# State-space layer: the softplus sum with an adding DMA, scans in place over four PSUM banks, and each read-out one unit later

## What is computed

```python
def _mamba(x, W_in, conv_w, conv_b, W_xproj, W_dt, b_dt, A_log, D_param, W_out):
    xp, z = jnp.split(x @ W_in.T, 2, axis=-1)           # 2 x 384 channels
    xc = silu(causal_conv4(xp) + conv_b)
    dt, Bt, Ct = jnp.split(xc @ W_xproj.T, [12, 28], axis=-1)
    dt = softplus(dt @ W_dt.T + b_dt)
    A = -jnp.exp(A_log)                                 # 384 x 16 states
    def step(h, inp):
        dt_t, B_t, C_t, x_t = inp
        h = jnp.exp(dt_t[..., None] * A) * h + (dt_t * x_t)[..., None] * B_t[:, None, :]
        return (h, jnp.einsum('bdn,bn->bd', h, C_t))
    _, ys = jax.lax.scan(step, h0, inputs)              # over the 128 tokens
    return ((ys + xc * D_param) * silu(z)) @ W_out.T
h = h + 0.5 * (_mamba(x) + _mamba(x[:, ::-1])[:, ::-1]) # x = layernorm(h)
```

## Time and profile before

| | us |
|---|---|
| median of 3 runs | 4825.98 (4822.94 to 4830.41) |
| profiled execution, its own time | 4824.94 |
| span of its trace | 4823.1 |
| PE busy | 4354.2 (90%) |
| DVE busy | 3395.9 (70%) |
| POOL busy | 3184.9 (66%) |
| ACT busy | 2378.0 (49%) |
| granted TensorE clock, mean | 0.959 of full |

### The profile page before, as it was taken

How to read it: one execution, slowest core, us unless ns; L and a number is a source line. 1 busy time by engine, 2 the same in 40 slices (tenths; PEclk the granted TensorE clock), 3 DMA queues, 4 the chain that set the end, 5 groups by cost and what they waited for, 6 DMA issues and landing times. The chain is left out here.

```text
span 4823.1 us, 62759 instructions
## 1 busy us (share of the span) xinstructions
PE 4354.2 (90%) x17088; PEld 2262.3 (47%) x17088; DVE 3395.9 (70%) x5016; ACT 2378.0 (49%) x4078; POOL 3184.9 (66%) x1637
## 2 busy tenths in 40 slices
PE   7999986996999999999999999999999975999994
PEld 4666644663334343343434334343433333666673
DVE  5677763111899999999999999999999985111114
ACT  3555542122665665656666565666656534122221
POOL 3222212441998999999999999999999951444441
PEclk9999997997999999999999999999999987999997
DMA  1000012342232233333223233222323221333456
GB/s 34 20 23 20 16 61 64 110 131 77 84 110 99 98 109 103 102 100 105 99 102 109 100 106 100 105 98 102 109 100 105 97 80 35 106 116 116 124 168 217
DMA packets 262442, 453.11 MB, mean 94 GB/s; under 512 B 38892, under 2 KB 175932, under 8 KB 262300
## 3 DMA queue, kind: packets, MB, share of 16 engines
q1 hardware_dynamic: 235776, 403.02, 25.3%
q0 software_dynamic: 23424, 48.00, 3.2%
q10 hardware_dynamic: 3100, 0.64, 0.1%
HBM read 409.75 MB, written 41.81 MB: 94 GB/s over the span
## 5 line engine op out<-in xcount | busy, mean ns | idle before, releaser
L1765 POOL TENSOR_TENSOR m_xh<-m_u,m_Bb 128x1536 f32<-128x1536 f32 x512 | 1753.0, 3457 | 223.4 <-DVE m_u L1639 223.0
L1694 PE MATMUL bank<-m_xh,ident 128*128 128x512 f32 x3072 | 1443.5, 605 | 26.3 <-POOL m_xh L1754 26.3
L1721 ACT ACTIVATE bank<-m_dt,m_Ac 128x508 f32<-128x508 f32 x1536 | 1019.2, 683 | 416.5 <-DVE bank L1736 281.1
L1736 DVE TENSOR_TENSOR_SCAN bank<-bank,m_xh 128x512 f32<-128x512 f32 x864 | 1060.1, 1227 | 36.3 <-ACT bank L1721 7.8
L1694 PEld LDWEIGHTS bank<-m_xh,ident 128*128 128x128 f32 x3072 | 568.5, 192 | 807.9 <-issue 730.7
L1736 DVE TENSOR_TENSOR_SCAN m_xh<-bank,m_xh 128x512 f32<-128x512 f32 x672 | 774.1, 1205 | 31.8 <-ACT bank L1721 27.7
L1754 POOL TENSOR_TENSOR m_xh<-m_xh,m_Cb 128x1536 f32<-128x1536 f32 x224 | 774.4, 3457 | 11.0 <-DVE m_xh L1736 10.6
L1745 DVE TENSOR_TENSOR m_xh<-bank,m_Cb 128x512 f32<-128x512 f32 x864 | 597.8, 692 | 69.3 <-DMA m_Cb<-BC_rows 23.9
L1204 ACT ACTIVATE f1t_h<-bank,f1t_b 128x512 f32<-128x512 f32 (+1 forms) x276 | 147.9, 587 | 509.7 <-PE bank L1234 509.7
L1553 PE MATMUL bank<-m_xp,m_dg 128*128 128x512 f32 x768 | 349.9, 598 | 3.2 <-ACT m_xc L1561 2.6
L1134 POOL DMA_INDIRECT rows_y<-f1t_y,f1t_home x142 | 139.9, 985 | 317.6 <-DVE f1t_y L1175 288.4
(11 more groups left out here) (366 smaller groups left out, 6138.1 us busy)
## 6 DMA issues: line engine op xcount, KB each, us to landing
m_Bb<-BC_rows SPq DMA_DIRECT2D x256, 512.0 KB, 4.7
m_Cb<-BC_rows SPq DMA_DIRECT2D x256, 512.0 KB, 3.9
f1t_w<-f_w SPq DMA_DIRECT2D x46, 576.0 KB
f1t_w1a<-f_w SPq DMA_DIRECT2D x46, 384.0 KB
f0t_w<-f_w SPq DMA_DIRECT2D x22, 576.0 KB
f1c_yg<-rows_y SPq DMA_DIRECT2D x16, 768.0 KB, 8.3
f1t_w1b<-f_w SPq DMA_DIRECT2D x92, 96.0 KB
f0t_w1a<-f_w SPq DMA_DIRECT2D x22, 384.0 KB
```

The source lines that it names most:

```text
L1694: mm = pe.matmul(bank[:, c, :], K.ident[:, :], xh[n % NX][:, c, :], start=False, stop=(d == 1 and n == NS - 1))
L1721: act.activation(o[:, :, lo:hi], seqs(dt[d][:, c, :])[:, :, lo:hi], ACT.Exp, scale=Ac[:, c, n:n + 1]).then_inc(s_dA, 1)
L1736: dve.tensor_tensor_scan(o, bank[:, 3 + p % 3, way], xh[n % NX][:, c, way], 0.0, ALU.mult, ALU.add).then_inc(s_h, 1)
L1765: pool.tensor_tensor(xh[n % NX][:, :, :], u[d][:, :, :], Bb[q % RB][:, n % QN, :].unsqueeze(1).to_broadcast([P, DC, TOK]), ALU.mult).then_ ...
```

## The change

- **Softplus sum.** A new step `pool_add`, behind the unit after `act_e` in POOL's program, issues one DMA that adds `e` to `r` in place (128 x 1536 float32, 768 KB). `pe_sp` sums three tiles, `w1, lw, r`, and waits for the DMA (`s_er`) before the first `r`.
- **Ring of four banks.** Decays go into banks 3 to 6 by the table `RING`. A DVE-read scan writes its states over its own decay, instead of into bank 6. A decay waits until the bank's last user is done (`released`): the scan, where POOL reads out; the read-out, where DVE does. The edge column is cleared again wherever states have overwritten it: 25 units in slot 0 and 31 in slot 1, for 3 and 3. Bank 6 is lent between units 7 and 15 of slot 0 to the rows that are added to H.
- **Read-outs one unit later.** DVE does scan p, then read-out p - 1.
- **Who reads out.** `BY_POOL` is a set per direction, 8 states in direction 0 and 6 in direction 1, for 7 and 7.
- **Gates last.** The gate matmuls of direction 1 move from behind units 10, 13, 16 to 23, 26, 31, after dt; the gate's SiLU moves to the next chain's `act_xc`. The output products wait for the projection instead of the gate copies.
- **POS** has other numbers nearly everywhere.

```diff
         POS = {
-            "y": (6, 9, 11), "pe_D0": (7, 11, 12), "pe_D1": (11, 23, 30), "pe_out": (17, 18), "out": (19, 22),
...
-            "act_xc": (19, 22), "act_e": (27, 32), "act_w1": (30, 34), "act_ln": (31, 35), "pe_sp0": (31, 36, 41),
-            "act_sp0": (36, 41, 42), "u0": (35, 39, 42), "pe_sp1": (38, 40, 42), "act_sp1": (39, 42, 43), "u1": (38, 40, 42),
+            "y": (6, 7, 9), "pe_D0": (14, 15, 17), "pe_D1": (6, 16, 25), "pe_out": (17, 18), "out": (14, 15),
...
+            "act_pj": (15, 10), "act_xc": (14, 8), "act_e": (23, 23), "act_w1": (23, 26), "act_ln": (26, 29),
+            "pe_sp0": (26, 36, 40), "act_sp0": (30, 39, 41), "u0": (34, 38, 41), "pe_sp1": (32, 38, 42), "act_sp1": (34, 38, 40),
+            "u1": (32, 37, 40),
         }
-        BY_POOL = (0, 3, 4, 7, 10, 12, 15)
+        BY_POOL = (0, 3, 4, 5, 10, 12, 13, 14), (0, 6, 9, 10, 11, 14)
+        RING = ((3, 4, 5, 6) * 2 + (3, 4, 5, 3, 4, 5, 3) + (6, 4, 5, 3) * 8 + (6,),
+                (4, 5, 3, 6, 4, 3, 5, 6) + (3, 4, 5, 6) * 10)
+        def released(act, g, d, p):
+            n, c = divmod(p, DC)
+            if n in BY_POOL[d]:
+                act.wait_ge(s_h, (g * 2 + d) * UNITS + p + 1)
+            else:
+                act.wait_ge(s_prv, dve_reads(g, d, n) + c + 1)
+            def pool_add(pool):
+                pool.wait_ge(s_e, s + 1)
+                stand_alone(pool, K.go)
+                pool.dma_start(r[:, :, :].rearrange("p c t -> p (c t)"), e[d][:, :, :].rearrange("p c t -> p (c t)"),
+                               accum_op=ALU.add).then_inc(s_er, 16)
             def pe_sp(pe, c):
                 if c == 0:
+                    if d == 1:
+                        pe.wait_ge(s_zc, g * DC + DC)
+                        stand_alone(pe, K.go)
                     pe.wait_ge(s_nc, s + 1)
...
-                for k, t in enumerate((r, e[d], w1[d], lw)):
-                    mm = pe.matmul(bank[:, front(c), :], K.ident[:, :], t[:, c, :], start=(k == 0), stop=(k == 3))
+                for k, t in enumerate((w1[d], lw, r)):
+                    if c == 0 and t is r:
+                        pe.wait_ge(s_er, (s + 1) * 16)
+                        stand_alone(pe, K.go)
+                    mm = pe.matmul(bank[:, front(c), :], K.ident[:, :], t[:, c, :], start=(k == 0), stop=(k == 2))
         def act_decay(act, g, d, p):
-            o = seqs(bank[:, 3 + p % 3, :])
+            o = seqs(bank[:, RING[d][p], :])
...
-            if later(g, d) or p >= 3:
-                act.wait_ge(s_h, U - 2)
-            if p < 3:
+            if d == 0 and p == ROWS_TO and not (isinstance(g, int) and g == NG - 1):
+                act.wait_ge(s_added, g * 2 + 4)
+            elif back == 0 or later(g, d):
+                released(act, g if db <= d and back < 2 else g - 1, db, pb)
+            if back or pb // DC not in BY_POOL[d] or d == 0 and p == ROWS_TO:
                 act.copy(o[:, :, edge:edge + 1], none[:, :].unsqueeze(2))
         def dve_scan(dve, g, d, p):
...
-                o = bank[:, 6, way]
-                if later(g, d) or p > 0:
-                    dve.wait_ge(s_prv, (g * 2 + d) * READS + reads(n) + c)
+                o = bank[:, RING[d][p], way]
                 def main(dve, g, d, p, end):
                     dve_scan(dve, g, d, p)
-                    if p // DC not in BY_POOL:
-                        dve_read(dve, g, d, p)
+                    if later(g, d) or p > 0:
+                        dve_read(dve, *((g, d, p - 1) if p > 0 else (g, 0, UNITS - 1) if d == 1 else (g - 1, 1, UNITS - 1)))
```

More of the change, by code:

```diff
@@ L1375, in mamba_phase @@
+            "act_rows": (11, 13), "rows": (12, 14), "stats": 14, "rstd": 18, "norm": 40,
[3 rows of a table added]
+            "act_pj": (15, 10), "act_xc": (14, 8), "act_e": (23, 23), "act_w1": (23, 26), "act_ln": (26, 29),
+            "pe_sp0": (26, 36, 40), "act_sp0": (30, 39, 41), "u0": (34, 38, 41), "pe_sp1": (32, 38, 42), "act_sp1": (34, 38, 40),
+            "u1": (32, 37, 40),
         }
         NB = 7
-        BY_POOL = (0, 3, 4, 7, 10, 12, 15)
-        ROWS_IN = 3
-        pool_reads = lambda n: sum(k < n for k in BY_POOL)
@@ L1380, in mamba_phase, with before_in_bank @@
-        reads = lambda n: DC * (n - pool_reads(n))
-        READS, POOL_READS = reads(NS), pool_reads(NS)
+        BY_POOL = (0, 3, 4, 5, 10, 12, 13, 14), (0, 6, 9, 10, 11, 14)
+        RING = ((3, 4, 5, 6) * 2 + (3, 4, 5, 3, 4, 5, 3) + (6, 4, 5, 3) * 8 + (6,),
+                (4, 5, 3, 6, 4, 3, 5, 6) + (3, 4, 5, 6) * 10)
+        ROWS_BANK, ROWS_FROM, ROWS_TO = 6, 7, 15
+        def before_in_bank(d, p):
+            b, back = RING[d][p], 0
+            while True:
+                p -= 1
+                if p < 0:
+                    p, d, back = UNITS - 1, 1 - d, back + 1
+                if RING[d][p] == b:
+                    return back, d, p
@@ L1382, in mamba_phase @@
+        of_pool = lambda d, n: sum(k < n for k in BY_POOL[d])
+        of_dve = lambda d, n: DC * (n - of_pool(d, n))
+        pool_reads = lambda g, d, n: g * (of_pool(0, NS) + of_pool(1, NS)) + d * of_pool(0, NS) + of_pool(d, n)
+        dve_reads = lambda g, d, n: g * (of_dve(0, NS) + of_dve(1, NS)) + d * of_dve(0, NS) + of_dve(d, n)
         of_q = lambda q: range(q * QN, (q + 1) * QN)
-        FIRST_POOL = [min((n % QN for n in of_q(q) if n in BY_POOL), default=None) for q in range(NQ)]
-        FIRST_DVE = [min((n % QN for n in of_q(q) if n not in BY_POOL), default=None) for q in range(NQ)]
+        first_pool = lambda d, q: min((n % QN for n in of_q(q) if n in BY_POOL[d]), default=None)
@@ L1385, in mamba_phase @@
+        first_dve = lambda d, q: min((n % QN for n in of_q(q) if n not in BY_POOL[d]), default=None)
         PW = P + 2 * (TAPS - 1)
@@ L1462, in act_rows @@
                         stand_alone(act, K.go)
-                        act.wait_ge(s_prv, g * 2 * READS + reads(ROWS_IN))
+                        released(act, g, 0, ROWS_FROM)
                 else:
                     act.wait_ge(s_added, gl * 2 + 1)
-                act.copy(bank[:, 6, 0:2 * C], z[:, 2 * i:2 * i + 2, :].rearrange("p j c -> p (j c)")).then_inc(s_copied, 1)
+                act.copy(bank[:, ROWS_BANK, 0:2 * C], z[:, 2 * i:2 * i + 2, :].rearrange("p j c -> p (j c)")).then_inc(s_copied, 1)
             def dve_rows(dve, i):
@@ L1565, in act_xc @@
                 act.activation(xc[d][:, :, :], xc[d][:, :, :], ACT.Silu).then_inc(s_xc, 1)
-                if d == 1:
-                    act.wait_ge(s_zc, g * DC + DC)
-                    act.activation(gz[:, :, :], gz[:, :, :], ACT.Silu).then_inc(s_gz, 1)
+                if d == 0 and not first:
+                    act_gz(act, g - 1)
                 act.preload_act_table_set("natural_log_exp_and_others")
@@ L1572, in pe_proj @@
                 pe.wait_ge(s_xc, s + 1)
[L1573 to L1576, removed]
                 for c in range(DC):
@@ L1590, in pe_dt @@
                     pe.wait_ge(s_pj, s + 1)
+                    if d == 1 and deep:
+                        stand_alone(pe, K.go)
+                        pe.wait_ge(s_out, g * 2)
                 elif not first:
@@ L1689, in pe_sum @@
         def pe_sum(pe, g, d, n, c):
-            if n not in BY_POOL:
-                pe.wait_ge(s_prv, (g * 2 + d) * READS + reads(n) + c + 1)
+            if n not in BY_POOL[d]:
+                pe.wait_ge(s_prv, dve_reads(g, d, n) + c + 1)
             elif c == 0:
-                pe.wait_ge(s_prp, (g * 2 + d) * POOL_READS + pool_reads(n + 1))
+                pe.wait_ge(s_prp, pool_reads(g, d, n + 1))
             mm = pe.matmul(bank[:, c, :], K.ident[:, :], xh[n % NX][:, c, :], start=False, stop=(d == 1 and n == NS - 1))
@@ L1843, in program @@
             before(eng)
+            end = {"pe": [], "act": [(POS["act_xc"][0], act_gz, (NG - 1,))], "dve": [], "pool": []}
             def group(g, last):
                 slot(eng, name, g, 0, chain(g, 1, norm=not last)[name], main, last)
-                slot(eng, name, g, 1, [] if last else chain(g + 1, 0)[name], main, last)
+                slot(eng, name, g, 1, end[name] if last else chain(g + 1, 0)[name], main, last)
             group(0, False)
@@ L1890, in main @@
                         pool_dBx(pool, *at_step(g, d, n + AHEAD))
-                    if c == 1 and (n - 1) % NS in BY_POOL and (n or later(g, d)):
+                    if c == 1 and (n - 1) % NS in BY_POOL[d if n else 1 - d] and (n or later(g, d)):
                         pool_read(pool, *at_step(g, d, n - 1))
@@ L1896, in last_read @@
                 def last_read(pool):
-                    if NS - 1 in BY_POOL:
+                    if NS - 1 in BY_POOL[1]:
                         pool_read(pool, NG - 1, 1, NS - 1)
```

33 lines of the change are left out of this document (21 added, 12 removed), and 6 rows, old and new, of the table POS.

## The result

| | before | after |
|---|---|---|
| median, us | 4824.46 (4820.66 to 4830.41, 4 runs) | 4720.85 (4719.26 to 4727.34, 4 runs) |
| span of the trace, us | 4823.1 | 4718.1 |
| granted TensorE clock, mean | 0.959 | 0.957 |

The ratio is 0.9783 [0.9771, 0.9794]: 104 us less, where 78 were forecast. The forecast group was 164.0 us long; it is 162.9.

The account below looks back on a forecast made before the run. DVE, occupied 163.1 of 168.9 us a group, was taken as tightest, PE and POOL close behind. Floors after of POOL 160.5, PE 163.8, DVE 156.2 gave 164.0; 4.9 x 16 groups = 78 us off 4824.9, so 4747 us, range 4690 to 4840.

Parts of the forecast that it names:

- What sets the pace: State-space layer: DVE, occupied 163.1 of 168.9 us a group, is tightest and sets the slot's pace; PE, POOL within 5 us.
- DVE's bubble: DVE scans and read-outs: independent neighbours cut a pair from 1.99 to 1.72 us, saving 12.7 a group, to 150.4.
- the rival: DVE's spacing stays unchanged by the drain rule, saving 0: group 168.9 us, 4825 us in all; chance 0.10.
- PE's three operands: PE's softplus sum: one identity matmul fewer per channel block, 6 a group, saving 5.2 us, to 156.8 of work.
- The new wait: PE before r: the adding transfer, landing in 7.0 us, comes 2.8 us late a group, in direction 0 only.
- the way to the issue: POOL, from the exponential's end to the adding DMA's issue: half a POOL product, 1.7 us.
- The sum: Group after the change: floors POOL 160.5, PE 163.8, DVE 156.2; taken as 164.0 us, 4.9 less than before.
- +3 us at the start: Start of the layer: the first chain shows the transfer openly, costing 3 us, offset by 3 at the end.
- a sign of being wrong: DVE waiting for ACT's decays more than 3 us a slot would show the prediction wrong.
- The late transfer: PE held by the adding DMA landing at 16.6 us: +10.1 us a group, 4987 us; chance 0.14.
- POOL at its floor: POOL sets the group at its floor of 160.5 us, giving 4690 us; chance 0.08.
- Sums held back: Held-back sums or the early output addition stop POOL or DVE 2.5 us a group more, 4786 us; chance 0.16.

Follow-up runs that it names:

- ring without the order: Changed banks, in-place scans, later read-outs and read-out sets, with the positions, gates and chain waits of the kernel before, four matmuls, no adding DMA: 4864.21 us.
- order without the ring: Kernel before with only the changed POS, gates last and their waits; three decay banks, read-out at once, 7 and 7 POOL read-outs, no DMA: 4910.0 us.
- without DMA, read-out sets of before: Changed kernel with no adding DMA, four softplus matmuls a block, and seven POOL read-outs in both directions instead of 8 and 6: 4773.47 us.
- without DMA: Changed kernel with the softplus sum as before, four matmuls a block and no adding DMA on POOL, all else as changed: 4699.98 us.
- DMA earlier: Changed kernel with the adding DMA one place earlier on POOL, in the exponential's own unit, ahead of the product of unit 24: 4695.49 us.
- DMA earlier, 13 read-outs: Changed kernel with the adding DMA one place earlier and 13 POOL read-outs a group, state 10 of direction 1 going to DVE: 4677.14 us.
- the same, read-out at once: Changed kernel with the adding DMA one place earlier, 13 POOL read-outs, and each DVE read-out right behind its own scan again: 4730.2 us.

## Why the prediction was right, and which of its steps failed

**What sets the pace: not borne out.** The prediction put DVE, occupied for 163 of 168.9 us, as the engine that sets the slot's pace. In the new kernel DVE does not set it: given 8 us back, it changed nothing (4723 for 4721). What the versions run into is PE, then POOL:

| version | us | group | PE work | PE's waits | POOL busy | DVE occupied |
|---|---|---|---|---|---|---|
| before | 4824 | 168.9 | 162.0 | 6.9 | 158.2 | 163.1 |
| ring without the order | 4864 | 171.8 | 163.3 | 8.4 | 158.2 | 150.5 |
| order without the ring | 4910 | 174.1 | 165.5 | 8.4 | 158.5 | 163.8 |
| without DMA, read-out sets of before | 4773 | 166.1 | 162.2 | 3.8 | 158.4 | 150.6 |
| without DMA | 4700 | 161.4 | 160.5 | 0.7 | 158.3 | 149.8 |
| changed | 4721 | 162.9 | 157.4 | 5.4 | 159.9 | 150.0 |
| DMA earlier | 4695 | 161.0 | 156.4 | 4.4 | 159.8 | 149.6 |
| DMA earlier, 13 read-outs | 4677 | 159.9 | 156.0 | 3.7 | 156.5 | 151.4 |
| the same, read-out at once | 4730 | 163.2 | 157.7 | 5.2 | 156.5 | 159.8 |

(All columns behind the second are us a group.) No engine was at its floor before. In the version without the DMA, the time that went is that of the waits between them: POOL's 10 us for `u`, PE's for the softplus operand, for the gate copies and for DVE's additions. In the change itself PE's work fell by 4.6 us and its waits by 1.5 only, since the wait for the DMA came in. I had read three engines within 5 us of each other as "the tightest sets the pace".

For the kernel before it stays open how much DVE counted. Relieved in the old order, its occupied time fell to 150.5 us and the group did not shorten (171.8); but that run also had the changed read-out sets, which go with the new order. In the new order, with the old sets, the same relief (163.8 to 150.6) comes with a group of 166.1 for 174.1. And no group of 162.9 us or less has room for the 163.1 us that DVE was occupied before. DVE had to be relieved, and that alone was not enough.

**How the gain comes about: not by parts.** The forecast added savings (DVE's 12.7, PE's 5.2). Measured alone, the ring with the changed read-out sets is worth +38 us and the order +83; order and ring together -51, and with the sets -125 (all without the DMA). So 73 of the 125 us hang on which states POOL reads out. The order issues the chain earlier (`act_e` behind units 23 and 23, for 27 and 32). That the fourth bank gives ACT the lead for it was my reading; the waits for decays do not show it, and the room that the ring gives DVE is a rival that no run separates from it. By itself the ring meets the old chain, where `u` is late and POOL stands still. What of the ring does it, the fourth bank, the scans in place or the later read-outs, was measured for the read-outs only: they are worth 3 us here (4723.38 against 4720.85, less than the intervals tell apart) and 53 in the best version.

**DVE's bubble: right.** Forecast 1.12 + 0.60 for a pair and 150.4 us occupied; measured 1.13 + 0.59 and 150.0. I had read an unchanged spacing out of the Trainium skill's "VectorE: DVE Perf Modes", section "The DRAIN you can't avoid". The section also says that a next op that is not held starts earlier. The rows fit that sentence and not the rival: the same two instructions stand 1.26 and 0.61 apart where one needs the other, and 1.13 and 0.59 where it does not. So needing the instruction just ahead did cost something, 0.15 us a pair. Against the order of before, where the next scan also needed bank 6 back, it is 1.99 - 1.72 = 0.27.

**PE's three operands: right, and given back.** 12 records a group went. The saving of 5.2 us (6 x 0.86) shows as 160.5 - 156.4 = 4.1 with the DMA one place earlier (what the missing 1.1 is, no row tells), and as 3.1 in the change. Lost clock fits the size of what is missing in the change. Just behind a wait of 3.53 us the next matmuls take about twice as long; PE's timeline of the changed kernel, and then three windows around it:

```profile
2481.09 1.99 PE L1666 MATMUL bank<-m_r,ident 128*128 128x512 f32 x2 [3.53 <-DMA m_r<-m_dt]
```

```profile
2471.00:2481.00 10.00, 6.55 (x16) 2.62 (x14) 9.99 (x11) 7.14 (x13) 10.00 (x5) 1.00 0.67 163
2481.00:2485.00 4.00, 3.91 (x5) 1.64 (x6) 0.99 (x2) 1.89 (x4) 3.85 (x3) 0.57 0.17 71
2485.00:2495.00 10.00, 10.00 (x25) 4.50 (x24) 10.00 (x11) 4.45 (x7) 10.00 (x3) 1.00 0.32 105
```

The granted clock is 0.57 in the four microseconds behind the gap, close to the lower level of 1.2 GHz, after a stretch in which PE was busy for 6.55 of 10 us; then it is whole again. That is 0.43 x 4.0 = 1.7 us of clock lost in this place. It does not follow every such wait. Of the twelve waits of 3.3 to 3.8 us in the window, nine are followed by it: in windows of 10 us from shortly before each wait's end the granted clock is 0.66 five times, 0.83 four times and 1.00 three times, one of these behind the 3.27 us shown further up. Together that is some 24 us of clock, 2.0 a group, and 5.2 - 2.0 = 3.2 stands beside the 3.1 measured.

**The new wait: right in kind, mis-sized.** Forecast 2.8 us a group, in direction 0 alone; measured 4.5, in both: over the twelve groups 3.3 to 3.8 us in direction 0 (3.5 in the mean) and 0.15 to 1.8 in direction 1 (0.9). The landing was right: 7.4 us at the median, forecast 7.0. The estimate of 3.8 us by the Trainium skill's "DMA: Bandwidth & Descriptors", section "Anatomy of one DMA — SWDGE (gpsimd) path", is about half of what this adding transfer takes. The term that failed is the way to the issue. I gave it half a POOL product, 1.7 us, behind the exponential's end. ACT, then POOL, in the changed kernel:

```profile
2305.52 1.48 ACT L1632 ACTIVATE m_dt<-m_dt 128x1536 f32<-128x1536 f32 x1
```

```profile
2305.15 3.46 POOL L1793 TENSOR_TENSOR m_xh<-m_xh,m_Cb 128x1536 f32<-128x1536 f32 x1
2308.56 3.46 POOL L1804 TENSOR_TENSOR m_xh<-m_u,m_Bb 128x1536 f32<-128x1536 f32 x1
2311.96 0.82 POOL L1651 DMA_DIRECT2D m_r<-m_dt  x1
2312.57 7.08 POOL L1804 TENSOR_TENSOR m_xh<-m_u,m_Bb 128x1536 f32<-128x1536 f32 x2
```

The exponential ends at 2307.00, the issue comes at 2311.96: 5.0 us, for what was left of one instruction and a whole second one. POOL is not free to take the DMA when its input is ready; it is full. In direction 1 two products stand between, 2389.04 to 2396.50: 7.5 us. One place earlier it is 1.5 us (2300.11 to 2301.63), near the 1.7 forecast, and there is no wait at all. In the rows above the transfer lets PE go 12.2 us behind the exponential (2319.21), 2.5 later than forecast, yet PE waits only 3.27 us for a forecast 2.8: the forecast also left out PE's own 1.9 us for the two matmuls that it does first (2314.06 to 2315.94), an error the other way. Per issue POOL lost 0.61 us (2311.96 to 2312.57), 0.69 in the other direction, forecast 1.0.

**The sum.** 164.0 came out 1.1 us too long, and its terms on PE were off both ways. Forecast were 156.8 of work, 4.2 of other waits and 2.8 for the transfer, 163.8; measured are 157.4, 0.9 and 4.5, 162.8. The forecast carried PE's other waits over from before, at 4.2 (6.9 less the 2.7 for the softplus operand), without asking what the change does to them. Nearly all are gone. That these 3.3 us too much outweigh the 1.7 us too little for the transfer and the 0.6 for the work is luck. POOL waits 1.3 us for `u`, not 3.5, and 0.9 for sums that were not in the sum; its floor is 159.9 for 160.5. The +3 us at the start did not come: the layer's first product starts at 1209.7 us, 1210.8 before.

ACT (109.2 for 111) was hidden. DVE's waits for decays rose from 2.3 to 78 / 12 = 6.5 us a group, where "a microsecond or two" more was forecast. That is 3.2 a slot, over the 3 that the prediction had named as a sign of being wrong; it lay in DVE's room. So the work of PE and POOL was forecast about right, the waits were not, and the reason given for the pace, DVE, was at most part of it.

**The rivals.** The late transfer is the one that is partly real: the DMA as placed costs 21 us net, without turning the sign. POOL at its floor, forecast at 4690, is what the DMA one place earlier reaches: 4695. Sums held back cost 10.3 / 12 = 0.9 us a group on POOL. What was missing among the rivals is that the parts could each be worth less than nothing alone.

## What to carry to other kernels

When several engines stand within a few per cent of each other, don't take the busiest one's occupied time as the pace: for each engine set work plus waits against the period, and test it by giving the suspect some time back. One that takes 8 us without a change had room, and the same edit can cost 53 us once the others have been shortened. A step that hands work to a full engine must be placed by when that engine reaches it, and one place was worth 25 us, from a loss of 21 to no loss. Changes that are laid out for each other, here the ring, the order and the read-out sets, are to be measured together too, since each alone can be slower.

## What the runs showed of the hardware that was not expected

- A gap of 3.5 us in PE's work, with much work on both sides, was followed by some 4 us at a granted clock of 0.57. Nine of twelve such gaps were, and three were not; without the gaps (the version without the DMA) the clock was 1.00 over all twelve groups.
- An adding DMA of 768 KB within SBUF lands 7.4 us (median of 32; 6.7 to 10.7) after its issue and holds POOL's next instruction for 0.61 to 0.69 us only. Behind it POOL's products are recorded as longer while their spacing stays as it was. In the changed kernel's POOL timeline:

```profile
2243.11 3.70 POOL L1804 TENSOR_TENSOR m_xh<-m_u,m_Bb 128x1536 f32<-128x1536 f32 x1
2246.50 3.70 POOL L1793 TENSOR_TENSOR m_xh<-m_xh,m_Cb 128x1536 f32<-128x1536 f32 x1
2249.89 3.70 POOL L1804 TENSOR_TENSOR m_xh<-m_u,m_Bb 128x1536 f32<-128x1536 f32 x1
```

Each is 3.70 us long and 3.39 from the next, where 3.46 and 3.40 stand elsewhere. So start-to-start times, not durations, are to be read there.
